# Storing tiles 6 to 13 of a recommendation head whole instead of tiles 9 to 11

## The reference

```python
all_embed = jnp.concatenate([users_emb_w[users], items_emb_w[items]], axis=1)
h = jax.nn.relu(all_embed @ w1.T + b1)
h = jax.nn.relu(h @ w2.T + b2)
cross = jax.nn.one_hot(items, NUM_ITEMS, dtype=h.dtype)
head_in = jnp.concatenate([cross, h], axis=1)
return jax.nn.sigmoid(head_in @ w_head.T + b_head)
```

## Time and profile before

| what | value |
|---|---|
| median of 3 runs | 96.99 us |
| lowest and highest | 96.24 and 97.76 us |
| the profiled execution | 95.91 us |
| its span, first to last instruction | 94.1 us |
| TensorE busy | 60.8 us (65%) |
| VectorE busy | 42.6 us (45%) |
| ScalarE busy | 40.4 us (43%) |
| GpSimd busy | 31.2 us (33%) |
| gathers (queue q0) | 10.77 MB, 36.2% of 16 DMA engines' span |
| SyncE's DMAs, nearly all stores (queue q1) | 10.29 MB, 28.6% |
| ScalarE's DMAs (queue q10) | 0.76 MB, 2.7% |
| stores | 20 of 312.5 KB, 3 of 625.0 KB, 6 of 256.0 KB, 3 of 113.0 KB (one of these by ScalarE) |

### The profile page before, as it was taken

How to read it: one execution, slowest core, us unless ns; L and a number is a source line. 1 busy time by engine, 2 the same in 40 slices (tenths; PEclk the granted TensorE clock), 3 DMA queues, 4 the chain that set the end, 5 groups by cost and what they waited for, 6 DMA issues and landing times.

```text
span 94.1 us, 915 instructions
## 1 busy us (share of the span) xinstructions
PE 60.8 (65%) x284; PEld 47.5 (50%) x284; DVE 42.6 (45%) x111; ACT 40.4 (43%) x91; POOL 31.2 (33%) x38
## 2 busy tenths in 40 slices
PE   3999848008400840000049999999999999999930
PEld 2433635007100810000048888888888888887820
DVE  5427430204030000000063659878788878789740
ACT  0537121400000200000052477887877877879860
POOL 2677787777777877772000000000000000000000
PEclk9999999975555588555555599999999999999999
DMA  0799888889999899888013135557656526757695
GB/s 9 209 360 322 260 266 240 245 292 323 290 277 279 268 348 330 277 266 279 1 49 136 60 125 223 219 200 276 245 192 241 197 84 264 281 234 304 266 370 187
DMA packets 8368, 21.86 MB, mean 232 GB/s; under 512 B 1580, under 2 KB 2476, under 8 KB 8364
## 3 DMA queue, kind: packets, MB, share of 16 engines
q0 software_dynamic: 2816, 10.77, 36.2%
q1 hardware_dynamic: 4972, 10.29, 28.6%
q10 hardware_dynamic: 576, 0.76, 2.7%
HBM read 11.56 MB, written 10.24 MB: 232 GB/s over the span
## 4 chain that ended last, share of the span: by engine, by line
PE 49%; another core or an unknown queue 31%; DVE 5%; DMA 4%; issue 4%; ACT 3%; ACTq 1%; DVEq 0%
PE acc L358 32%; DMA w_hid_f<-w_hiddenT 4%; PE ps_h L354 4%; PE ps_h L350 3%; DVE rows L242 2%; PE ps_h L349 2%; PE acc L391 2%; PE ps_x L338 2%; DVE w_hid_lo L211 1%; PE acc L389 1%; PE acc L388 1%; PE acc L386 1%; ACT rows L308 1%; ACT w_hid_hi L289 1%
## 5 line engine op out<-in xcount | busy, mean ns | idle before, releaser
L242 DVE TENSOR_TENSOR rows<-acc,rows 128x625 f32<-128x625 f32 (+2 forms) x35 | 25.9, 749 | 11.3 <-remote 4.5
L308 ACT ACTIVATE rows<-rows 128x625 f32<-128x625 f32 (+2 forms) x35 | 23.3, 678 | 0.9 <-DVE rows L242 0.8
L225 DVE CAST embT<-ps_x 128x128 fp32r<-128x128 f32 x16 | 4.7, 292 | 31.2 <-remote 24.5
L349 PE MATMUL ps_h<-embT,w1T_hi 128*128 128x128 f32 x16 | 4.5, 278 | 21.0 <-DVE embT L225 19.6
L179 POOL DMA_INDIRECT rows<-item_rows,idx x16 | 15.4, 960 | 6.0 <-issue 4.6
L183 POOL DMA_INDIRECT rows<-user_rows,idx x16 | 15.1, 946 | 4.9 <-issue 4.9
L298 ACT ACTIVATE h2T_hi<-ps_h,b_sb 128x128 fp32r<-128x128 f32 x15 | 5.5, 369 | 24.8 <-remote 18.4
L349 PEld LDWEIGHTS ps_h<-embT,w1T_hi 128*128 128x128 f32 x16 | 3.3, 209 | 22.8 <-DVE embT L225 20.6
L294 ACT ACTIVATE h1T<-ps_h,b_sb 128x128 f32<-128x128 f32 x16 | 5.9, 368 | 20.1 <-remote 12.2
L358 PE MATMUL acc<-bias_parts,bias_sel 128*128 128x512 f32 (+1 forms) x42 | 11.7, 387 | 0.0
L358 PE MATMUL acc<-w_hid_hi,h2T_lo 128*128 128x512 f32 (+1 forms) x39 | 11.6, 410 | 0.0
(11 more groups left out here) (39 smaller groups left out, 56.6 us busy)
## 6 DMA issues: line engine op xcount, KB each, us to landing
probs<-rows SPq DMA_DIRECT2D x20, 312.5 KB
probs<-rows SPq DMA_DIRECT2D x3, 625.0 KB
probs<-rows SPq DMA_DIRECT2D x6, 256.0 KB
w_hid_f<-w_hiddenT ACTq DMA_DIRECT2D x1, 625.0 KB
rows<-item_rows,idx POOLq DMA_INDIRECT x16
rows<-user_rows,idx POOLq DMA_INDIRECT x16
probs<-rows SPq DMA_DIRECT2D x2, 113.0 KB
probs<-rows ACTq DMA_DIRECT2D x1, 113.0 KB
```

The lines of the kernel that those rows point to most:

```text
L225: nc.vector.tensor_copy(embT[:], ps_x[:, 0:P]).then_inc(s_embT, 1)
L242: nc.vector.tensor_tensor(logits(t, c, n), acc[t % SLOTS][:, c:c + n], logits(t, c, n), ALU.add).then_inc(s_sum, 1)
L308: nc.scalar.activation(logits(t, c, n), logits(t, c, n), ACT.Sigmoid).then_inc(s_prob, 1)
L349: nc.tensor.matmul(ps_h[:, 0:P], w1T_hi[:], embT[:], start=True, stop=False)
```

## The change

The tuple of tiles that are stored whole grows from three to eight. No other line differs.

```diff
-STORED_WHOLE = (9, 10, 11)
+STORED_WHOLE = (6, 7, 8, 9, 10, 11, 12, 13)
```

## The result

Over 20 runs each, the changed kernel takes 97.29 us in the median (96.30 to 99.28) and the kernel before 96.35 us (95.33 to 97.76). The ratio is 1.0111 with a 95% interval of 1.0084 to 1.0137, so the change costs about 1.1 us, or 0.8 to 1.3 us.

The account below looks back on a forecast made before the run. The stores of the last three tiles form one nearly unbroken train whose end sets the span. Terms 0 + 0 + 0 + 0.64, about +0.6 us on the 96.99 us median, give 97.6 us, range 96.4 to 98.6 us.

Parts of the forecast that it names:

- hidden case: Rival at the program's end: idle DMA time swallows tile 13's whole 0.76 us push; 97.0 us, chance 0.10.
- Fewer issues: On SyncE's queue: five issues of 0.33 us and five waits go, hidden behind its waits for sigmoids; 0.
- Tiles 6, 7, 8 and 12: Their first halves leave later, but their whole stores finish before the next tile's store needs the queue; cost 0.
- Tile 13: First half joins the last store train: +0.76 us, less a 0.12 us gap before tile 15's second bank, +0.64 us.
- Larger rows: In store transfers: a whole tile takes 1.57 us against 1.62 us for two halves, saving 0.05 us a tile.
- straggler: Rival in the last train: an instruction fetch holds up one DMA engine, end 2.1 us later, 99.1 us; chance 0.08.
- price per store: Rival on the store path: each store pays 0.9 us lag, five fewer save 4.5 us, 92.5 us; chance 0.05.
- early disturbance: Rival in the first 48 us: the shorter SyncE program shifts time about 2.5 us either way, 94.5 or 99.5 us; chance 0.07.

Follow-up runs that it names:

- broken train: Kernel before with tile 14 not stored, tile 13 in halves or whole; one run each, last data 1.79 and 1.78 us behind the last store's issue.
- three halves late: Kernel before with all four half-tile stores of tiles 12 and 13 waiting for tile 13's last sigmoid; median 99.53 us against 96.22 us, ratio 1.0423.
- held tile 13: Kernel before with tile 13 still in two stores, the first also waiting for the second half's sigmoid; median 97.22 us, ratio 1.0151.
- third series: Tile 14's stores delayed 67.02 us, no tile whole 67.16 us, kernel before again 66.92 us, changed kernel again 66.47 us; kernel before 67.07 us over 35 runs.
- first two series: Follow-up runs varying which tiles are stored whole, delayed or unstored, each beside new runs of the kernel before: medians 96.72 us, then 96.22 us.

## Why the prediction was right, and what it missed

**The sign and the place were right.** The forecast of no change within 2%, slower by 0.6 us, stands against a measured 1.1 us (0.8 to 1.3). That the median of 97.29 us lies so near the forecast of 97.6 us is in part luck. The forecast started from the 96.99 us of three runs, and 20 runs gave 96.35 us, 0.64 us lower; the change was larger than forecast by 0.3 us in the medians. The two errors have opposite signs. The range of 96.4 to 98.6 us also held the hidden case at 97.0 us, so it is the lag that tells them apart. Each step:

- *Fewer issues, 0.* SyncE still waits 30.4 us for sigmoids. Shown by its waits only.
- *Tiles 6, 7, 8 and 12, 0.* Shown: with these whole and tile 13 in halves the lag is 1.82 us, as before.
- *Tile 13, +0.64 us.* Shown four times over: lags of 2.40, 2.42, 2.41 and 2.50 us with its first half late, 1.82, 1.82 and 1.81 us with it early. That is +0.59 us, where the sum had +0.76 - 0.12 = +0.64 us. With a broken train the cost is gone (1.79 and 1.78 us), with three halves late instead of one it is +2.57 us.
- *Larger rows, 0.05 us a tile.* In the first condition this is right: SyncE's DMAs take 28.6% of 94.1 us, or 26.9 us, before and 27.8% of 95.9 us, or 26.7 us, after (26.6 us in the second trace of the changed kernel), 0.2 to 0.3 us less over five tiles. The held tile 13 has 0.08 us more lag in two halves than in one store. In the third series the same count gives 0.12 us or more a tile.
- *The straggler and the price per store* did not show. The fixed cost of about 2 us per DMA that the Trainium skill, "DMA: Bandwidth & Descriptors", section "Anatomy of one DMA", gives for GpSimd's path is not paid once per store here: 31 stores and 27 both give a lag of 1.82 us, and 30 and 26 give 2.42 and 2.41 us.
- *The early disturbance* did not show. In the eight traces of kernels that store every tile, the last issue comes at 90.53 to 92.06 us where tile 13's first half is late and at 91.40 to 92.75 us where it is not, on average at 91.7 and 91.9 us.

**What was missed is 0.35 to 0.5 us in size.** The measured 1.1 us is more than the 0.59 us of the train. It may be chance: pooled over the result and the first two series, the means are 96.39 us (48 runs of the kernel before) and 97.33 us (26 runs of the changed one), 0.94 us apart with a standard error of 0.19 us, so 0.59 us is just inside two of these. (The medians are 0.91 us apart.) The other candidate is the rest behind the last data. It is 0.81 and 1.37 us for the kernel before, 1.54 us with tiles 6 to 12 whole, and 1.64, 1.18, 1.09, 1.34 and 1.34 us for the kernels with tile 13's first half late. The first pair of profiles, 0.81 against 1.64 us, looked like a cost of the change; the 1.54 us of a kernel with an undelayed train speaks against that, and the spread inside one kernel is half a microsecond. On average the rest is 1.24 us in the three undelayed traces and 1.32 us in the five others. **Whether the completions are on average later in the changed kernel stays open**: eight traces don't resolve 0.3 us.

The prediction also took the condition of the machine for given. None of its rivals was that the DMA engines could be full from 20 us on, and there the change is a small gain.

No version that was run beats the kernel before clearly in the first condition: tiles 6 to 12 whole with tile 13 in halves equals it (means 96.42 and 96.53 us). In the condition of the third series it was not run.

## What to carry to other kernels

Coalescing stores costs what it makes late. In the condition of the prediction that was paid only by the tile whose store began the unbroken train at the end of the program. So look for the last idle moment of the DMA engines: what could leave before it should, and what leaves well before it was merged at no cost in the lag. Where the DMA engines were full from 20 us on, the merged kernel was 0.7% faster, but splitting all tiles lost nothing measurable, so a saving per merged store is not shown.

## What the runs showed of the hardware

The same program took 96.2 to 96.7 us (medians) beside the result and in the first two series, and 67.1 us in the third. At 96 us TensorE's granted clock is at half of full speed (1.2 of 2.4 GHz) for long stretches between 14 and 55 us, and VectorE and ScalarE stand for up to 20.22 us with a releaser that the trace does not name, while the gathers run. At 67 us the clock is full until TensorE has finished, and the stall is not there. No run here shows what causes the stall, or whether the clock fell because TensorE stood still. The difference of 29 us is nearly thirty times the size of the change.

The time from the last data to the end of the span varied from 0.81 to 1.64 us in ten traces of the first condition, without a tie to the kernel, and was 0.83 to 0.88 us in the four of the second. A sustained train of stores moved 378 GB/s over 6.7 us, with rows of 2,500, 2,048 and 904 bytes, where a single half-tile store of 2,500-byte rows moved 395 GB/s of the engines' busy time. From SyncE's issue to the first data it took 0.8 to 0.9 us on an empty queue (the earlier trace rows, tile 11).
